# A fused attention block on one core: TensorE's stages in another order, products with v in pairs, and q and k rotated before they are divided by their roots

## The chip, the core and the metric

The kernel runs on one core of one Trainium2 chip. Its engines work side by side, each through its own queue in order, and wait for one another by semaphores: TensorE (PE, with its weight loads as PEld), VectorE (DVE), ScalarE (ACT), GpSimd (POOL) and SyncE (SP), which issues DMAs. The metric is the device time in microseconds (us); lower is better.

## The reference

For 16 sequences of 512 rows with 512 channels, `x` gets an attention branch added. EPS is 1e-6 and there are 16 heads of e = 32 channels.

```python
h = _layernorm(x)
mod = jax.nn.silu(time) @ mod_w + mod_b
shift, scale, gate = jnp.split(mod, 3, axis=-1)
h = h * (scale + 1.0) + shift
qkv = (h @ w_qkv).reshape(B, T, 3, H, e).transpose(2, 0, 3, 1, 4)
q, k, v = (qkv[0], qkv[1], qkv[2])
q = _apply_rope(_layernorm(q, q_norm_w), position)
k = _apply_rope(_layernorm(k, k_norm_w), position)
scores = jnp.einsum('bhqe,bhke->bhqk', q, k) / jnp.sqrt(jnp.asarray(e, q.dtype))
attn = jax.nn.softmax(scores, axis=-1)
o = jnp.einsum('bhqk,bhke->bhqe', attn, v)
o = o.transpose(0, 2, 1, 3).reshape(B, T, D)
return x + o @ w_out * gate
```

Only the first half of each head's channels is rotated by `_apply_rope`.

## The kernel before

The work is cut in two ways. A tile `n` (0 to 63) is 128 rows of one sequence; a group `g` (0 to 63) is 4 heads of one sequence, so a sequence has 4 tiles and 4 groups. There is no scheduler: each engine's program is a loop over stages `s` = 0 to 63, written out by hand, and semaphore counts tie the engines together. Stage `s` works on group `s` by key, on group `s + 1` by query, on tiles ahead and on a tile behind:

- `transpose_c`, `transpose_qk`: the maxima of group `s`, and q and k of group `s + 1`, turned on PE.
- `scores_by_key(s, t)`, t = 0 to 3 (here key(t)): 16 matmuls on row quarters of the array (32 rows each, four at a time) into the banks SA and SM. ACT takes the exponentials from SM first and then from SA (`key_exponentials`, two halves).
- `scores_by_query(s + 1, t)` (here query(t)): 4 such matmuls into SM and MB; DVE takes the maxima of SM, then of MB (`maxima`). SM is shared by query(t) and key(t), so query(t) waits for the first half of the exponentials of key(t), and key(t + 1) waits for the first maximum of query(t).
- `weigh_values(s, t)` (here value(t)): v times the exponentials, on column quarters of the array (128 rows by 32 columns, four at a time) into O. `add_over_keys(s - 1)` (here sums) has the same form, with ones for v, into Y. Each is four matmuls that the trace shows as eight records.
- `project`: q and k of tile `s + 6`, v of tile `s + 4`, 12 matmuls each with the full array, into the one bank Y; `project_out(s - 5)`: the output product, 12 full matmuls, also into Y. `transpose_x(s + 6)` turns the next input tile into SA; ACT and DVE split it in a high and a low part (`x_high`, `x_low`), and key(2), which writes SA next, waits for them.
- For q and k, ACT copies the projection (`move_qk`) and squares it (`square`); DVE sums the squares (`square_sums`), finds the inverse roots and multiplies (`normalize_qk`); then POOL rotates the result (`rotate`, three operations for q and three for k).
- The exponentials are summed over key tiles by two accumulating DMAs, issued by POOL (`add_keys(s, 1)`, `add_keys(s, 3)`), and one POOL addition (`sum_keys(s - 1)`), which the sums on PE then use.

In PE's stage a product with v stands behind each `scores_by_key`, and projections are cut so that a few of their matmuls stand ahead of each `scores_by_query`. In the last stages (`late(s + 1)`, which holds for s from 58 to 62) nothing is left to project for q and k, and the scores by query are made in halves that use MB alone:

```python
if late(s + 1):
    scores_by_query_half(s + 1, 3, 0)
weigh_values(s, 2)
```

There the sums take two parts of the exponentials on PE, and POOL has no `sum_keys`; from group 60 on a spare buffer for them is used (`homes`).

## Time and profile before

| | us |
|---|---|
| median of 3 runs | 1730.7 |
| lowest and highest run | 1730.56, 1736.18 |
| the profiled execution | 1735.34 |
| its span, first to last instruction | 1733.5 |
| PE busy in it | 1660.1 (96%) |
| DVE busy | 1178.0 (68%) |
| ACT busy | 996.9 (58%) |
| POOL busy | 949.5 (55%) |

Busy time of PE is the union of its matmuls' records. A wait between two of them, or a gap that nothing explains, doesn't always show as idle time, since a record's end reaches over the next one's start; so the argument below goes by the distance from one start to the next.

### The profile page before, as it was taken

The page shows a single profiled execution, that of the slowest core. Times are in us where ns is not written, and L with a number is a line of the kernel's source. Part 1 is how long each engine was busy: PE and PEld are TensorE (multiplying, and loading weights), DVE is VectorE, ACT ScalarE, POOL GpSimd, SP SyncE. Part 2 cuts the span into 40 slices and gives each one's busy share as a digit, 9 for nine tenths or more (in the row PEclk, how much of TensorE's full clock was granted, in tenths as well). Part 3 has the DMA queues.
Part 4 walks back from the last instruction along what each step waited for, and adds up shares of the span by engine and source line. Part 5 has one row for each costly group of instructions (what it writes and reads, how often), then busy time and mean ns, then how long its engine had stood idle before and what let it go on. Part 6 is the DMA issues. An engine that isn't in the chain of part 4 may idle for free.

```text
span 1733.5 us, 31073 instructions
## 1 busy us (share of the span) xinstructions
PE 1660.1 (96%) x11870; PEld 955.4 (55%) x11870; DVE 1178.0 (68%) x1541; ACT 996.9 (58%) x1484; POOL 949.5 (55%) x766
## 2 busy tenths in 40 slices
PE   5979999999999999999999999999999999999887
PEld 2745555555555555555555555555555555554434
DVE  8767766676776677666677667667666767765552
ACT  3446666556656655656655665565665566565542
POOL 0535656656565665665665656566566565655322
PEclk9989999999999999999999999999999999999999
DMA  6035454555555555555555454554645546454543
GB/s 214 26 68 110 112 117 107 129 122 122 122 116 125 119 123 124 114 122 128 123 116 135 105 133 116 119 132 106 146 108 116 134 104 140 110 113 107 116 104 110
DMA packets 55417, 204.26 MB, mean 118 GB/s; under 512 B 6872, under 2 KB 6872, under 8 KB 39144
## 3 DMA queue, kind: packets, MB, share of 16 engines
q0 software_dynamic: 18144, 132.13, 38.5%
q1 hardware_dynamic: 37128, 70.14, 12.2%
q8 instruction: 98, 1.61, 0.4%
q14 instruction: 47, 0.39, 0.1%
HBM read 53.25 MB, written 16.88 MB: 40 GB/s over the span
## 4 chain that ended last, share of the span: by engine, by line
PE 82%; DVE 12%; issue 3%; DMA 1%; ACT 1%; POOL 1%; SPq 0%; DVEq 0%; POOLq 0%; ACTq 0%
PE O L481 13%; PE SA L462 12%; PE Y L374 9%; PE Y L370 9%; PE Y L367 9%; DVE cst L1088 6%; PE SM L419 6%; PE Y L496 4%; PE Y L358 4%; PE MB L402 3%; PE Y L380 3%; PE SA L466 2%; DVE hT_lo L1071 2%; PE SM L462 1%; PE SA L440 1%
## 5 line engine op out<-in xcount | busy, mean ns | idle before, releaser
L1088 DVE TENSOR_REDUCE cst<-SM 128x2 fp32r<-128x1024 f32 x236 | 289.4, 1226 | 321.9 <-PE MB L419 321.9
L1334 POOL TENSOR_TENSOR probs<-probs 128x2048 f32<-128x2048 f32 x59 | 271.3, 4599 | 253.4 <-DMA probs<-probs 253.4
L844 ACT ACTIVATE probs<-SM 128x1024 f32<-128x1024 f32 x253 | 259.3, 1025 | 243.6 <-PE SM L466 236.8
L1307 POOL TENSOR_TENSOR pair_part<-rows,rope_pair 128x256 f32<-128x256 f32 x128 | 120.0, 938 | 318.4 <-DVE rows L1065 317.5
L1088 DVE TENSOR_REDUCE cst<-MB 128x2 fp32r<-128x1024 f32 x236 | 287.1, 1216 | 0.0
L481 PE MATMUL O<-probs,vals 128*32 128x512 f32 x2024 | 271.5, 608 | 0.0
L846 ACT ACTIVATE probs<-SA 128x1024 f32<-128x1024 f32 x253 | 257.9, 1019 | 0.0
L741 ACT ACTIVATE rows<-Y 128x512 f32<-128x512 f32 x121 | 72.5, 599 | 232.9 <-PE Y L374 232.9
L370 PE MATMUL Y<-wqkv_hi,hT_lo 128*128 128x512 f32 x716 | 194.3, 393 | 0.4 <-DVE hT_lo L1071 0.4
L374 PE MATMUL Y<-wqkv_lo,hT_hi 128*128 128x512 f32 x716 | 193.2, 391 | 0.0
L1077 DVE SCALAR_TENSOR_TENSOR qk_lo<-MB,pass_w,qk_hi 128x512 fp32r<-128x512 f32 x128 | 90.5, 747 | 131.2 <-ACT qk_hi L777 131.1
L367 PE MATMUL Y<-wqkv_hi,hT_hi 128*128 128x512 f32 x540 | 174.2, 431 | 0.0
L1326 POOL DMA_DIRECT2D probs<-probs x123 | 107.5, 874 | 116.6 <-ACT probs L846 100.1
L370 PEld LDWEIGHTS Y<-wqkv_hi,hT_lo 128*128 128x128 f32 x716 | 134.2, 188 | 32.7 <-DVE hT_lo L1071 0.8
L374 PEld LDWEIGHTS Y<-wqkv_lo,hT_hi 128*128 128x128 f32 x716 | 134.4, 188 | 30.2
L462 PE MATMUL SA<-qk_hi 32*128 32x512 f32 x512 | 128.7, 495 | 20.1 <-DVE hT_lo L1071 11.2
L462 PE MATMUL SM<-qk_hi 32*128 32x512 f32 x512 | 128.3, 497 | 0.0
L419 PE MATMUL SM<-qk_hi 32*128 32x512 f32 x472 | 119.1, 499 | 7.1 <-DVE cst L1088 4.8
L1312 POOL TENSOR_TENSOR rows<-rows,rope_same 128x256 f32<-128x256 f32 x128 | 114.2, 892 | 10.0
L419 PE MATMUL MB<-qk_hi 32*128 32x512 f32 x472 | 118.8, 500 | 0.0
L367 PEld LDWEIGHTS Y<-wqkv_hi,hT_hi 128*128 128x128 f32 x540 | 87.5, 188 | 53.3 <-issue 43.9
L419 PEld LDWEIGHTS SM<-qk_hi 32*128 32x128 f32 x472 | 44.0, 182 | 117.4 <-issue 111.9
(236 smaller groups left out, 3573.2 us busy)
## 6 DMA issues: line engine op xcount, KB each, us to landing
probs<-probs POOLq DMA_DIRECT2D x123, 1024.0 KB, 7.7
xin<-in_x_dram SPq DMA_DIRECT2D x62, 256.0 KB, 7.5
xres<-in_x_dram SPq DMA_DIRECT2D x60, 256.0 KB, 2.6
out_dram<-xres SPq DMA_DIRECT2D x60, 256.0 KB, 5.4
shift_scale<-mod_rows SPq DMA_DIRECT2D x15, 512.0 KB, 3.8
gate<-mod_rows SPq DMA_DIRECT2D x16, 256.0 KB, 5.9
rows<-in_L_cond_mod_w_dram SPq DMA_DIRECT2D x2, 1024.0 KB, 8.9
probs<-in_L_cond_w_qkv_dram SPq DMA_DIRECT2D x2, 1024.0 KB, 13.2
```

The lines of the kernel that those rows point to most:

```text
L367: pe.matmul(bank, x_hi[:, k, :], wqkv_hi[:, k, cols], start=(k == 0), stop=False)
L370: pe.matmul(bank, x_lo[:, k, :], wqkv_hi[:, k, cols], start=False, stop=False)
L374: mm = pe.matmul(bank, x_hi[:, k, :], wqkv_lo[:, k, cols], start=False, stop=(k == DT - 1))
L419: mm = pe.matmul(qm_bank(i), qk_hi[r, g % 2, 0, cols], qk_hi[r, g % 2, 1, :], start=True, stop=True)
L462: pe.matmul(s_bank(i), a[r, ring, 1, cols], c[r, ring, 0, :], start=(a is qk_hi and c is qk_hi), stop=False)
L481: mm = pe.matmul(O[head_rows(i), :], vals[:, b % 2, t, E * h:E * (h + 1)], key_probs(g, t)[:, i, :], start=(t == 0), stop=(t == TT - 1), s ...
L844: act.activation(a[:, 2:4, :], SM[:], ACT.Exp).then_inc(s_exp, 1)
L846: act.activation(a[:, 0:2, :], SA[:], ACT.Exp).then_inc(s_exp, 1)
L1088: dve.tensor_reduce(heads[:, 2 * half:2 * half + 2, 0], bank[:], AX.X, ALU.max, negate=True).then_inc(max_out, 1)
L1307: pool.tensor_tensor(pair_part[:].rearrange("p h (i two) -> p h i two", two=2), swapped, rope_pair[:, t, j, :].rearrange("p (i two) -> p i ...
L1312: pool.tensor_tensor(r[:, :, 0:R], r[:, :, 0:R], rope_same[:, t, j, :].unsqueeze(1) .to_broadcast([P, H, R]), ALU.mult).then_inc(rope_step, 1)
L1334: pool.tensor_tensor(total, total, part, ALU.add).then_inc(keys_summed, 1)
```

## The change

On PE, for stages up to 57, value(0) and value(1) now stand one behind the other with the sums right behind them, and value(2) and value(3) stand together near the end of the stage; value(3) no longer waits for the next stage. The output product is no longer cut: its 12 matmuls and then `transpose_x` follow key(1), ahead of query(1). The v and q projections are cut after 5 of 12 matmuls, the k projection after 8. Stages from 58 on make the scores by query in one piece into SM and MB, as all other stages do; the halves, the spare buffer and the Y bank for `transpose_x` are gone, and only groups 62 and 63 have their sums in more than one part.

POOL rotates q as soon as its squares are taken (`squared`), and DVE's `normalize_qk` waits for the rotation, where POOL had waited for `normalize_qk`. `transpose_qk` waits for `qk_norm`. On POOL, `rotate(s + 5, 0)` stands ahead of `sum_keys(s - 1)`, `rotate(s + 5, 1)` behind it, and then `add_keys(s, 1)`. On DVE the gate's product stands ahead of the maxima of query(1), and `x_low` between these. On ACT `log_sums` stands ahead of the exponentials of key(2).

```diff
+    def late(s):
+        return s > NT - 7
...
+            def project_part(n, j, bank, first, last):
                 x_hi, x_lo = x_buffers(n)
                 cols = slice(j * D, (j + 1) * D)
+                for m in range(first, last):
+                    k, (x, w) = m % DT, ((x_hi, wqkv_hi), (x_lo, wqkv_hi), (x_hi, wqkv_lo))[m // DT]
+                    mm = pe.matmul(bank, x[:, k, :], w[:, k, cols], start=(m == 0), stop=(m == 3 * DT - 1))
+                if last == 3 * DT:
+                    mm.then_inc((q_done, k_done, v_done)[j], 1)
...
             def transpose_qk(g, j):
                 b, i = g // NG, g % NG
                 if i == 0:
-                    pe.wait_ge(rope_step, 6 * (TT * b + 3) + 3 * (j + 1))
+                    pe.wait_ge(qk_norm, TT * b + TT)
...
+                begun = 5 if s > 0 and not late(s - 1) else 0
+                if begun:
+                    project_part(s + 4, 2, Y[:], 0, begun)
+                if group(s + 1):
                     scores_by_query(s + 1, 0)
...
+                        pe.wait_ge(o_low, n + 1)
                         pe.wait_ge(v_out, s + 5)
+                        project_out(n, Y[:], 0, 12)
+                        transpose_x(s + 6)
+                        scores_by_query(s + 1, 1)
...
+                    weigh_values(s, 0)
+                    weigh_values(s, 1)
+                    if s > 0:
...
+                        add_over_keys(s - 1)
...
+                    pe.wait_ge(h_hi, s + 7)
+                    pe.wait_ge(h_lo, s + 7)
+                    project_part(s + 6, 0, Y[:], 0, 5)
+                    scores_by_query(s + 1, 2)
+                    project_part(s + 6, 0, Y[:], 5, 12)
...
                     pe.wait_ge(raw_out, raw_count(s + 6, 0))
+                    project_part(s + 6, 1, Y[:], 0, 8)
                     scores_by_query(s + 1, 3)
+                    weigh_values(s, 2)
+                    weigh_values(s, 3)
+                    project_part(s + 6, 1, Y[:], 8, 12)
...
             def normalize_qk(n):
                 dve.wait_ge(newton_step, NEWTON * (n + 1))
-                dve.wait_ge(squared, 2 * n + 2)
+                dve.wait_ge(rope_step, 6 * (n + 1))
...
             def rotate(n, j):
-                pool.wait_ge(qk_norm, n + 1)
+
+                pool.wait_ge(squared, 2 * n + j + 1)
...
-                if s > 0 and not late(s - 1):
-                    sum_keys(s - 1)
-                add_keys(s, 1)
                 if tile(s + 5):
                     rotate(s + 5, 0)
                 if s > 0:
-                    scale_o(s - 1)
+                    sum_keys(s - 1)
                 if tile(s + 5):
                     rotate(s + 5, 1)
+                add_keys(s, 1)
+                if s - 5 >= 0 and not late(s):
+                    add_residual(s - 5)
+                if s > 0:
+                    scale_o(s - 1)
```

The lists below give the order in which an engine's instructions are queued (line, operation, output and inputs, number of instructions). First PE in a steady stage, from the end of key(3) (L466) to the next stage's transposes (L440, after the change L406). Before, L481 is a product with v, L358, L367, L370 and L374 are the k projection, L419 is query(3):

```order
L466 MATMUL SM<-cT,ones_r 128x512 x2
L481 MATMUL O<-probs,vals 32x512 x4
L358 MATMUL Y<-wqkv_hi,hT_hi 128x512
L419 MATMUL SM<-qk_hi 128x512 x2
L419 MATMUL MB<-qk_hi 128x512 x2
L367 MATMUL Y<-wqkv_hi,hT_hi 128x512 x3
L370 MATMUL Y<-wqkv_hi,hT_lo 128x512 x4
L374 MATMUL Y<-wqkv_lo,hT_hi 128x512 x4
L440 MATMUL SA<-ident_r,cst 128x128 x4
```

The same place after the change, where L432 is the end of key(3), L339 any projection, L396 a query and L447 a product with v:

```order
L432 MATMUL SM<-cT,ones_r 128x512 x2
L339 MATMUL Y<-wqkv_hi,hT_hi 128x512 x4
L339 MATMUL Y<-wqkv_hi,hT_lo 128x512 x4
L396 MATMUL SM<-qk_hi 128x512 x2
L396 MATMUL MB<-qk_hi 128x512 x2
L447 MATMUL O<-probs,vals 32x512 x8
L339 MATMUL Y<-wqkv_lo,hT_hi 128x512 x4
L406 MATMUL SA<-ident_r,cst 128x128 x4
```

One block of eight products with v stands behind query(3), and four matmuls of the k projection behind that, where eleven had been. The second place is PE in the same stage from the output product to key(2), after the change (L357 output product, L331 `transpose_x`, L462 sums, L428 key(2)):

```order
L357 MATMUL Y<-wout_hi,o_lo 128x512
L331 MATMUL SA<-ident,xin 128x128 x4
L396 MATMUL SM<-qk_hi 128x512 x2
L396 MATMUL MB<-qk_hi 128x512 x2
L447 MATMUL O<-probs,vals 32x512 x8
L462 MATMUL Y<-probs,ones_r 32x512 x4
L428 MATMUL SA<-qk_hi 128x512 x2
```

Before, the input's transposes stood inside the output product with eight of its matmuls behind them, then came key(2), and the sums and value(1) behind it. The third place is POOL's queue in one steady stage. Before (L1334 `sum_keys`, L1326 an accumulating DMA, L1307, L1312 and L1315 a rotation, L1340 `scale_o`, L1320 the residual, L1345 `output_low`):

```order
L1334 TENSOR_TENSOR probs<-probs 128x2048
L1326 DMA probs<-probs 128x2048
L1307 TENSOR_TENSOR pair_part<-rows,rope_pair 128x256
L1312 TENSOR_TENSOR rows<-rows,rope_same 128x16x16
L1315 TENSOR_TENSOR rows<-rows,pair_part 128x16x16
L1340 TENSOR_TENSOR oT<-oT,sum_inv 128x4x128
L1307 TENSOR_TENSOR pair_part<-rows,rope_pair 128x256
L1312 TENSOR_TENSOR rows<-rows,rope_same 128x16x16
L1315 TENSOR_TENSOR rows<-rows,pair_part 128x16x16
L1326 DMA probs<-probs 128x2048
L1320 TENSOR_TENSOR xres<-xres,gated 128x512
L1345 TENSOR_TENSOR o_lo<-oT,o_hi 128x512
```

And after the change (rotation L1261, L1266, L1269; `sum_keys` L1288; DMA L1280; residual L1274; `scale_o` L1294; `output_low` L1299):

```order
L1261 TENSOR_TENSOR pair_part<-rows,rope_pair 128x256
L1266 TENSOR_TENSOR rows<-rows,rope_same 128x16x16
L1269 TENSOR_TENSOR rows<-rows,pair_part 128x16x16
L1288 TENSOR_TENSOR probs<-probs 128x2048
L1261 TENSOR_TENSOR pair_part<-rows,rope_pair 128x256
L1266 TENSOR_TENSOR rows<-rows,rope_same 128x16x16
L1269 TENSOR_TENSOR rows<-rows,pair_part 128x16x16
L1280 DMA probs<-probs 128x2048
L1274 TENSOR_TENSOR xres<-xres,gated 128x512
L1294 TENSOR_TENSOR oT<-oT,sum_inv 128x4x128
L1280 DMA probs<-probs 128x2048
L1299 TENSOR_TENSOR o_lo<-oT,o_hi 128x512
```

A rotation now stands on either side of `sum_keys`, and the first DMA issue behind both rotations.

## Rows read from the trace of the kernel before

**Rows 1.** Windows: length, busy of PE, PEld, DVE, ACT, POOL; PE clock; DMA share; GB/s

```profile
217.30:1571.90 1354.60, 1343.44 (x9754) 778.12 (x9753) 938.94 (x1215) 816.05 (x1219) 808.75 (x637) 1.00 0.53 120
1642.91:1669.06 26.15, 22.43 (x153) 10.27 (x153) 11.91 (x11) 11.69 (x15) 5.59 (x6) 0.80 0.46 102
1692.20:1733.50 41.30, 31.68 (x217) 17.48 (x215) 12.46 (x17) 11.71 (x15) 7.57 (x6) 0.91 0.37 109
```

**Rows 2.** Timeline of PE, stage 31: start us, length, what, idle before

```profile
907.40 0.46 PE L440 MATMUL SA<-ident_r,cst 128*128 128x128 f32 x4
...
908.74 0.50 PE L462 MATMUL SA<-qk_hi 32*128 32x512 f32 x2
...
909.88 1.06 PE L481 MATMUL O<-probs,vals 128*32 128x512 f32 x8
910.88 0.73 PE L358 MATMUL Y<-wqkv_hi,hT_hi 128*128 128x512 f32 x2
911.54 0.50 PE L419 MATMUL SM<-qk_hi 32*128 32x512 f32 x2
...
911.98 0.74 PE L367 MATMUL Y<-wqkv_hi,hT_hi 128*128 128x512 f32 x2
...
917.25 0.50 PE L419 MATMUL SM<-qk_hi 32*128 32x512 f32 x2
...
918.26 0.60 PE L350 MATMUL SA<-ident,xin 128*128 128x128 f32 x4
918.61 0.48 PE L380 MATMUL Y<-wout_lo,o_hi 128*128 128x512 f32 x1
918.93 0.40 PE L380 MATMUL Y<-wout_hi,o_lo 128*128 128x512 f32 x1
...
920.32 0.39 PE L380 MATMUL Y<-wout_hi,o_lo 128*128 128x512 f32 x1
920.91 0.50 PE L462 MATMUL SA<-qk_hi 32*128 32x512 f32 x2 [0.20 <-DVE hT_lo L1071]
...
922.04 1.07 PE L496 MATMUL Y<-probs,ones_r 128*32 128x512 f32 x8
922.92 1.04 PE L481 MATMUL O<-probs,vals 128*32 128x512 f32 x8
923.89 0.50 PE L419 MATMUL SM<-qk_hi 32*128 32x512 f32 x2
...
932.92 0.29 PE L440 MATMUL SA<-ident_r,cst 128*128 128x128 f32 x2
```

**Rows 3.** Waits of PE from 217 to 1571 us: us in total, times, longest

```profile
PE SA L462 <- DVE hT_lo L1071: 11.2, 53, 0.2
```

**Rows 4.** Timeline of ACT and DVE, stage 31; line L1065's durations (ns min/median/max)

```profile
909.99 1.02 ACT L844 ACTIVATE probs<-SM 128x1024 f32<-128x1024 f32 x1
910.91 1.02 ACT L846 ACTIVATE probs<-SA 128x1024 f32<-128x1024 f32 x1
...
912.10 1.23 DVE L1088 TENSOR_REDUCE cst<-SM 128x2 fp32r<-128x1024 f32 x1 [0.81 <-PE MB L419]
913.24 1.22 DVE L1088 TENSOR_REDUCE cst<-MB 128x2 fp32r<-128x1024 f32 x1
...
L1065 DVE TENSOR_TENSOR rows<-rows,rstd x64: 1224/1224/1227, 48.0 to 1589.1; 128x1024 f32<-128x1024 f32 x64
```

**Rows 5.** Timeline of POOL in stage 31, and line L1307's durations (ns min/median/max)

```profile
905.25 0.87 POOL L1326 DMA_DIRECT2D probs<-probs  x1 [0.67 <-ACT probs L846]
...
912.45 4.60 POOL L1334 TENSOR_TENSOR probs<-probs 128x2048 f32<-128x2048 f32 x1 [3.77 <-DMA probs<-probs]
...
L1307 POOL TENSOR_TENSOR pair_part<-rows,rope_pair x128: 725/740/1194, 49.4 to 1594.0; 128x256 f32<-128x256 f32 x128
```

**Rows 6.** Timeline of PE in the last stages

```profile
1642.91 0.46 PE L440 MATMUL SA<-ident_r,cst 128*128 128x128 f32 x3 [1.33 <-DVE cst L1096]
...
1702.45 0.70 PE L380 MATMUL Y<-wout_hi,o_lo 128*128 128x512 f32 x1 [2.12 <-POOL o_lo L1345]
```

More of the change, by code:

```diff
@@ L48, in group, with probs_buffer @@
         return 0 <= g < NS
-    def late(g):
-        return group(g) and g > NT - 6
-    homes, spare = [(0, 1, 2, 3)], TT
-    for g in range(1, NS):
-        b = homes[-1]
-        if g < NS - NG:
-            homes.append((b[1], b[3], b[0], b[2]))
-        else:
-            homes.append((spare, b[1], b[3], b[0]))
-            spare = b[2]
+    def late(s):
+        return s > NT - 7
+    PROBS_RING = (0, 1, 3, 2)
+    def probs_buffer(g, t):
+        return PROBS_RING[(PROBS_RING.index(t) + g) % TT]
     def raw_count(n, j):
@@ L420, in scores_by_query @@
                 mm.then_inc(qm_done, 1)
-            def scores_by_query_half(g, t, half):
-                n = TT * g + t
-                if t == 0 and half == 0:
-                    pe.wait_ge(qk_low, 2 * g + 2)
-                pe.wait_ge(max_out, 2 * n + half)
-                cols = slice(t * P, (t + 1) * P)
-                for i in range(2):
-                    r = head_rows(2 * half + i)
-                    mm = pe.matmul(MB[:, i, :], qk_hi[r, g % 2, 0, cols], qk_hi[r, g % 2, 1, :], start=True, stop=True)
-                mm.then_inc(qm_half, 1)
             def transpose_c(g):
@@ L451, in scores_by_key @@
                     pe.wait_ge(s_exp, 2 * n)
-                if t == 0 or (group(g + 1) and not late(g + 1)):
+                if t == 0 or group(g + 1):
                     pe.wait_ge(max_out, 2 * (n + TT - 1) + 1)
-                if t == 2 and g >= 5 and tile(g + 6):
+                if t == 2 and tile(g + 6):
                     pe.wait_ge(h_hi, g + 7)
@@ L586, in _ @@
                 scores_by_key(s, 0)
-                if s > 0:
+                if late(s - 1):
                     weigh_values(s - 1, 3)
@@ L932, in _ @@
                     guess_roots(s + 7)
+                if s > 0 and (s == LAST or not late(s)):
+                    log_sums(s - 1, Y[:])
                 key_exponentials(s, 2, 0)
-                if s > 0:
+                key_exponentials(s, 2, 1)
+                if late(s) and s < LAST:
                     log_sums(s - 1, Y[:])
-                key_exponentials(s, 2, 1)
                 if s > 0:
@@ L1079, in low_qk, with maximum @@
                                          ).then_inc(qk_low, 1)
-            def maxima(g, t):
+            def maximum(g, t, half):
                 dve.wait_ge(qm_done, TT * g + t + 1)
@@ L1086, in maxima @@
                 heads = cst[:, t, :].rearrange("p (h e) -> p h e", e=E)
[L1087 to L1096 removed]
+                dve.tensor_reduce(heads[:, 2 * half:2 * half + 2, 0], (SM, MB)[half][:], AX.X, ALU.max, negate=True
                                   ).then_inc(max_out, 1)
+            def maxima(g, t):
+                maximum(g, t, 0)
+                maximum(g, t, 1)
             def apply_gate(n, bank, to):
@@ L1367, in _ @@
                 if s > 0:
-                    scale_o(s - 1)
+                    sum_keys(s - 1)
                 if tile(s + 5):
                     rotate(s + 5, 1)
+                add_keys(s, 1)
+                if s - 5 >= 0 and not late(s):
+                    add_residual(s - 5)
+                if s > 0:
+                    scale_o(s - 1)
+                if late(s):
+                    add_residual(s - 5)
                 if s == LAST - 1:
```

244 lines of the change are left out of this document (91 added, 153 removed).

## The prediction

> **What bounds the kernel now.** I read the windows by stage first. From 217.3 to 1571.9 us run stages 5 to 57, 53 stages with all parts: 1354.6 / 53 = 25.56 us each, PE busy 1343.4 of 1354.6 us, its granted clock 1.00, DVE at 69%, ACT and POOL at 60% [rows 1]. PE sets the pace, and a stage is worth what its matmuls take plus what lies between them. So I read PE's timeline by distances between starts [rows 2]. Twelve transposes take 1.34 us (907.40 to 908.74), a scores-by-key block 1.14 (to 909.88), one product with v that stands alone 1.00 (to 910.88), two full matmuls between two blocks of other shape 0.66 (to 911.54), a scores-by-query block 0.44 (to 911.98). Seven output matmuls in a row begin from 918.93 to 920.32, 0.23 each. So two full ones cost 2 x 0.23 + 0.20: a run of full matmuls pays 0.20 for its two edges, of which the first interval shows 0.09 (918.61 to 918.93). The sums followed by value(1) show that a column block costs 0.88 when another follows (922.04 to 922.92), not 1.00; with a query behind it, 0.97. The list of waits says that in these 53 stages PE waits for one thing only: key(2) for `x_low`, 11.2 us in 53 times [rows 3]. Around it, 920.32 to 920.91 is 0.59; less 0.23 and a closing edge of 0.09 leaves 0.27 for that wait [rows 2].
>
> The last stages are different. Stages 58 to 62 take 120.3 us (1571.9 to 1692.2), stage 63 with the close 41.3 [rows 1]. PE idles there: 1.33 us before a stage's transposes for the maxima of a half query, 2.12 us in stage 63 for POOL's `output_low` [rows 6]. In stage 61, behind such idle time, the granted clock averages 0.80, so 40% of the stage is at 1.2 instead of 2.4 GHz, and the stage takes 26.15 us where stage 62 takes 23.1 with one output product more [rows 1].
>
> **The change, steady stages.** The number of matmuls stays. What changes are the edges and one wait.
>
> - Column blocks: five pieces (four products and the sums) stand in four groups now, in two after. Two more pieces cost 0.88 instead of 1.00: 0.23 gained. That a piece in a pair costs 0.88 is read from sums then value; value then value writes the same bank O and isn't in the rows: bounds 0 and 0.24.
> - Runs of full matmuls: seven before, seven after (v 5 and 7, output 12 with the turned input, q 5 and 7, k 8, k 4 with the transposes). No gain.
> - The turned input: it stands inside the output product before, 918.26 to 918.93 for four transposes and a matmul, so 0.44. At the end of the run it costs four times 0.11 (1.34 / 12) and perhaps a second edge: I take 0.05 lost, bounds 0 and 0.10.
> - The wait for `x_low`: the turned input now has query(1), both values and the sums behind it before key(2), 3.1 us. ACT's and DVE's halves of it took until 0.2 past the need with eight output matmuls (2.3 us) as cover, and half a query's maxima stand ahead of it instead of a whole query's. 0.27 gained, bounds 0.20 and 0.28.
>
> Sum: 0.23 - 0.05 + 0.27 = 0.45 a stage, 25.1 us, times 53 = 24 us. With the bounds it is 5 to 29.
>
> **What hides the rest.** A stage after, from its transposes: key(0) 1.3, query(0) 3.8, key(1) 6.1, output 7.2, turned input 10.1, query(1) 10.7, value(0) 11.1, sums 12.9, key(2) 13.8, query(2) 16.3, key(3) 18.6, query(3) 21.7, value(2) 22.2, rest of k 24.1, end 25.1. The waits that could take hold:
>
> - query(0) and query(2) need SM's exponentials, 2.27 us after the key's start (908.74 to 909.99 + 1.02) [rows 2, 4]. The key and five matmuls take 1.14 + 5 x 0.23 + 0.20 = 2.49: 0.2 to spare, less than now, where the product with v stands there.
> - The next transposes need both maxima of query(3), 2.92 us after its start (911.54 to 913.24 + 1.22) [rows 2, 4]; it has 0.44 + 0.88 + 1.00 + 1.02 = 3.3. Key(3) needs the first maximum of query(2), 1.8 after 16.3, so 18.1 against 18.6. If these covers were 0.5 us shorter each, each would cost the difference.
> - POOL. The second DMA is issued when value(2) is done, at 23.2, and lands 7.2 us on (905.25 to 912.45) [rows 5], at 5.4 of the next stage; `sum_keys` 4.6 us ends at 10.0; the k rotation, three operations of about 0.8, at 12.5. The sums on PE want it at 12.9 from `sum_keys` alone, 2.9 to spare. DVE wants the rotation for `normalize_qk`: now 4.9 us after query(1) (917.25 to 922.12, where its 1.22 us start); after, at about 15.0. So 2.5 to spare. It then ends at 16.2, ahead of query(2)'s maxima at 16.9. The q rotation lies at the stage's start, before the DMA lands. The first DMA is issued at about 12.5 and is needed by the next stage's exponentials at 27.7; the residual, `scale_o` and the second issue follow with room. SP's stores hang on the residual, which comes earlier than now.
>
> Stages 0 to 4 lack the output product, so query(1) waits for exponentials in the new order too; the idle time moves and I count 0 to 1 us gained. At the start the rotations run ahead of the roots instead of behind them, with transposes waiting for the later of the two: 0.
>
> **The change, last stages.** Query pieces whole. From a key's start the query comes at 2.3 (exponentials), and the next key at the earliest 1.84 behind the query (SM's first maximum) [rows 4]. In stages 60 and 61 the output product comes in halves of 6 x 0.23 + 0.20 = 1.58, which cover that for t = 0 and 1: 1.34 + 2 x (2.3 + 0.44 + 1.58) + (2.3 + 1.84) + (2.3 + 2.97) = 19.4. Stages 58 and 59 have a v projection and a whole output product: 21.2 and 22.2. Stage 62 adds an output product that waits for POOL, whose `output_low` is queued behind `scale_o` and the residual: 22. Together 104 instead of 120.3. But each of these stages ends in 2.5 us without a matmul (2.97 less 0.44), longer than today's gap. In today's stage 61 the half clock cost some 3 us for 10 us at 1.2 GHz; I put 8 us on five stages. Stage 63: the output product of tile 59 now stands ahead of key(1) and waits there for the same POOL chain, but the sums are out of the close; 1 to 2 us gained. Sum 120.3 + 41.3 - 104 - 8 - 40 = 10 us gained, bounds 2 (clock down most of the time, stage 63 worse) and 18 (no clock loss).
>
> **Total.** 24 + 10 + 0.5 = 34.5 off the profiled execution's 1735.3 gives 1701. That execution lies 4.6 above the median of the runs, 1730.7; taken off the median, 1696.
>
> **The rivals.**
>
> - *The edges only move.* A product in a pair pays its edge all the same, or the 0.2 us covers fail and give the 0.45 back. Then only the last stages gain: 1720. For it: 0.2 us is thin. Against: 0.88 is measured. Chance 0.10.
> - *The last stages gain nothing*, since PE idles longer and is at 1.2 GHz for most of them: 1730.7 - 24 = 1706. For it: 0.80 in stage 61. Chance 0.10.
> - *Slower: the rotation behind `sum_keys` comes late.* POOL waits for the DMA, then adds, then rotates k, and DVE, in order, holds `normalize_qk` and query(2)'s maxima behind it; key(3) on PE waits. It costs from 3.6 us of delay on (2.5 of POOL, 0.6 on DVE, 0.5 before key(3)), and outweighs the gain 0.65 us later still (0.45 a stage, and 10 / 53 for the tail). With the DMA landing 5 us later than its 7.2, a stage would lose 1.4 - 0.45: 50 - 10 = 40 us, 1771. Against: POOL waits 3.77 us for this DMA today, and nothing on PE shows it. Chance 0.06.
> - *DVE is held up by POOL.* L1307 takes 0.74 us, but up to 1.19 beside some DVE work [rows 5], so the two do touch. In the new order `normalize_qk` at 15.0 meets the residual's addition on POOL. It has 0.6 + 0.5 us to spare; held 1.5 us by it, each stage gives 0.4 back: 1730.7 - 10 - 3 = 1718. Against: L1065 never took over 1.227 us in 64 times [rows 4], though it met few POOL operations. Chance 0.06.
>
> By the Trainium skill, "SBUF — State Buffer", section "Who interferes with whom", a DVE instruction with two SBUF inputs and a GpSimd instruction that reads SBUF exclude each other for the whole of whichever came first; by it this last rival would be the rule, wherever the two meet, and the rotations would get shorter beside maxima, which read PSUM. The trace agrees in that L1307's time varies.
>
> **How the numbers follow.** The forecast has 0.68. The range is 1685 to 1712: it takes in the tail's bounds, a steady gain from 0.25 to 0.55 a stage, and the second rival; the first, third and fourth lie outside. A difference under 0.5% (9 us) can't be told from none by these runs. Faster by more: forecast, second rival, most of the first and fourth, 0.90. Slower: 0.05. Between: 0.05.
>
> **What would show it.** A steady stage of 25.1 us; value(0) to value(1) 0.88; no wait of key(2) for `x_low`; POOL's k rotation ending near 12.5; stages 60 and 61 near 20, with the clock under 1.00. I'd be wrong if query(0) or query(2) waited for ACT in each stage, if DVE waited for `rope_step`, or if the last stages ran at 1.2 GHz throughout.

## The result and the profile after

The changed kernel takes 1721.36 us (median of 5 runs, 1719.39 to 1723.68) against 1732.28 for the kernel before (5 runs): ratio 0.9937, 95% interval 0.9921 to 0.9954. It is faster by 0.6%, where 2% was forecast, and 1721 lies above the range's end of 1712. The profiled execution spans 1719.1 us against 1733.5.

The same stretches as in [rows 1], from the windows of the changed kernel. The first window runs over stages 5 to 57, the next over stage 61, then stage 62, then stage 63 with the close, the last over stages 58 to 63 together. Columns: length, busy of PE, PEld, DVE, ACT, POOL, PE clock, DMA share, GB/s.

```profile
227.25:1561.39 1334.14, 1327.30 (x9753) 788.32 (x9752) 969.92 (x1215) 815.52 (x1219) 773.93 (x637) 1.00 0.54 123
1624.45:1645.69 21.24, 17.68 (x144) 8.56 (x144) 11.53 (x12) 11.85 (x15) 10.07 (x6) 0.92 0.67 143
1651.43:1676.66 25.23, 22.07 (x156) 12.48 (x157) 11.53 (x11) 11.86 (x15) 10.26 (x7) 0.86 0.60 126
1676.66:1719.10 42.44, 32.33 (x217) 18.07 (x215) 12.45 (x17) 11.70 (x15) 7.56 (x6) 0.89 0.29 90
...
1561.39:1719.10 157.71, 129.54 (x965) 68.48 (x963) 74.00 (x79) 73.59 (x96) 63.22 (x43) 0.90 0.49 112
```

Stages 5 to 57 begin at 227.25 instead of 217.30 [rows 1]. So three parts make up the difference: everything ahead of stage 5 became 10.0 us longer, the 53 steady stages 20.5 shorter (1354.60 to 1334.14), the last stages with the close 3.9 shorter (120.3 + 41.3 to 157.7). That is -14.4. Nearly 1 us of this only changed place: value(3) now stands in its own stage, so stage 0 holds eight records of products with v more (32 for 24) and stage 58 eight fewer.

**The steady stages.** Most of them do what was forecast. This is PE's timeline of stage 22 (start us, length, what), the counterpart of [rows 2].

```profile
652.66 0.46 PE L406 MATMUL SA<-ident_r,cst 128*128 128x128 f32 x4
...
662.52 0.40 PE L357 MATMUL Y<-wout_hi,o_lo 128*128 128x512 f32 x1
662.75 0.60 PE L331 MATMUL SA<-ident,xin 128*128 128x128 f32 x4
663.29 0.49 PE L396 MATMUL SM<-qk_hi 32*128 32x512 f32 x2
...
663.72 1.92 PE L447 MATMUL O<-probs,vals 128*32 128x512 f32 x16
665.46 1.04 PE L462 MATMUL Y<-probs,ones_r 128*32 128x512 f32 x8
666.43 0.50 PE L428 MATMUL SA<-qk_hi 32*128 32x512 f32 x2
...
677.68 0.46 PE L406 MATMUL SA<-ident_r,cst 128*128 128x128 f32 x4
```

The stage is 25.02 long. Two products with v take 1.74 (663.72 to 665.46), 0.87 each, and key(2) at 666.43 carries no idle time. But 11 of the 53 stages are longer than 25.2, up to 26.24; their excess over 25.02 is 7.6 us, and 8.1 over all 53. The waits of PE in these stages name what comes late: the maxima, ahead of a key block, 11 times.

```profile
PE SA L428 <- DVE cst L1053: 6.8, 11, 1.1
```

What holds the maxima is seen on DVE and POOL. The timeline of stage 22 first (25.02), then of stage 23 (25.77):

```profile
665.99 1.58 POOL L1274 TENSOR_TENSOR xres<-xres,gated 128x512 f32<-128x512 f32 x1
666.71 0.91 DVE L1000 TENSOR_SCALAR half_var<-stats 128x33 f32<-128x33 f32 x1
...
668.21 1.22 DVE L1031 TENSOR_TENSOR rows<-rows,rstd 128x1024 f32<-128x1024 f32 x1
...
685.01 4.62 POOL L1288 TENSOR_TENSOR probs<-probs 128x2048 f32<-128x2048 f32 x1 [4.05 <-DMA probs<-probs]
...
692.12 2.02 DVE L1004 TENSOR_TENSOR newton<-newton,half_var 128x33 f32<-128x33 f32 x1
692.51 1.58 POOL L1274 TENSOR_TENSOR xres<-xres,gated 128x512 f32<-128x512 f32 x1
...
694.41 1.23 DVE L1031 TENSOR_TENSOR rows<-rows,rstd 128x1024 f32<-128x1024 f32 x1
...
696.92 0.49 PE L428 MATMUL SA<-qk_hi 32*128 32x512 f32 x2 [0.67 <-DVE cst L1053]
```

The root steps work on 128 x 33 numbers and take 0.17 to 0.20 us. L1000 takes 0.91 here, and ends at 667.62 with POOL's residual addition (667.57). In stage 23 the second accumulating DMA lands late, `sum_keys` begins at 7.3 into the stage instead of 5.8, POOL's chain shifts by 1.5, and a later root step, L1004, ends with the residual (694.14 and 694.09) after 2.02. Then `normalize_qk` (L1031) starts at 16.7 into the stage instead of 15.6, query(2)'s maxima are late and key(3) waits 0.67. In ten of the 11 long stages `sum_keys` begins 6.6 to 7.8 into the stage; in stage 30 it is on time (5.8), and the residual is 0.8 late because POOL's first DMA issue waits for value(1).

**The start.** DVE and POOL in the timeline at the preparation of the fourth tile (tile 3), where PE then idles:

```profile
68.52 4.54 POOL L1305 TENSOR_TENSOR wout_lo<-probs,wout_hi 128x2048 fp32r<-128x2048 f32 x1
68.65 4.46 DVE L1006 SCALAR_TENSOR_TENSOR rstd<-newton,rstd 128x33 f32<-128x33 f32 x1
...
75.03 1.22 PE L339 MATMUL Y<-wqkv_hi,hT_lo 128*128 128x512 f32 x2 [4.64 <-DVE hT_lo L1037]
```

The subtraction for `wout_lo` used to begin at 75.24, behind a rotation that waited for this very division. Now nothing holds it back, it begins 0.13 us ahead of the last root step, and the root step ends with it, after 4.46 us. Stage 0's first transposes follow at 102.08 instead of 95.84. Stages 0 and 1 then take 27.64 and 25.59 instead of 25.46 and 24.0. In stage 1 the granted clock is 0.93 where it was 1.00. In stage 0 it is no lower than before (0.76 and 0.75), though it is at half in places (the window below); there value(3) accounts for nearly 1 us, and the rest of the 2.2 isn't taken apart.

```profile
98.50:105.30 6.80, 4.02 (x24) 3.12 (x28) 3.34 (x5) 1.97 (x3) 0.00 (x0) 0.50 0.00 0
```

### The profile page after: what moved, and what is told of

Read it like the earlier page. It is cut to its first block, busy times and chain, and to the rows that moved or that the text cites. A ratio compares the mean times of both kernels' runs of the same rounds, so it can differ in the third digit from the quotient of the medians.

```text
span 1719.1 us, 31069 instructions
## 1 busy us (share of the span) xinstructions
PE 1641.9 (96%) x11846; PEld 967.8 (56%) x11846; DVE 1210.6 (70%) x1541; ACT 997.1 (58%) x1484; POOL 926.3 (54%) x769
## 4 chain that ended last, share of the span: by engine, by line
PE 83%; DVE 8%; issue 4%; DMA 3%; POOL 1%; ACT 1%; SPq 0%; POOLq 0%; ACTq 0%; DVEq 0%
PE Y L339 31%; PE O L447 12%; PE SA L428 12%; PE Y L357 10%; PE SM L396 6%; PE MB L379 3%; PE SA L432 3%; PE Y L462 2%; DVE cst L1053 2%; PE SA L331 2%; DMA probs<-probs 1%; DVE newton L1004 1%; PE SA L406 1%; DVE rows L1031 1%; DMA probs<-in_L_cond_w_qkv_dram 1%
## 5 line engine op out<-in xcount | busy, mean ns | idle before, releaser
L1053 DVE TENSOR_REDUCE cst<-SM 128x2 fp32r<-128x1024 f32 x256 | 313.7, 1225 | 183.5 <-PE MB L396 183.0
L1288 POOL TENSOR_TENSOR probs<-probs 128x2048 f32<-128x2048 f32 x62 | 285.4, 4604 | 200.1 <-DMA probs<-probs 200.1
L1053 DVE TENSOR_REDUCE cst<-MB 128x2 fp32r<-128x1024 f32 x256 | 311.3, 1216 | 0.0
L1280 POOL DMA_DIRECT2D probs<-probs x126 | 110.1, 873 | 308.9 <-PE O L447 298.5
L447 PE MATMUL O<-probs,vals 128*32 128x512 f32 x2048 | 253.9, 610 | 0.0
L339 PE MATMUL Y<-wqkv_hi,hT_lo 128*128 128x512 f32 x716 | 226.8, 412 | 4.6 <-DVE hT_lo L1037 4.6
L339 PE MATMUL Y<-wqkv_hi,hT_hi 128*128 128x512 f32 x716 | 213.5, 420 | 0.0
L339 PE MATMUL Y<-wqkv_lo,hT_hi 128*128 128x512 f32 x716 | 202.0, 404 | 0.0
L1294 POOL TENSOR_TENSOR oT<-oT,sum_inv 128x512 f32<-128x512 f32 x63 | 83.5, 1326 | 169.5 <-ACT sum_inv L781 169.5
L339 PEld LDWEIGHTS Y<-wqkv_lo,hT_hi 128*128 128x128 f32 x716 | 130.4, 188 | 75.7 <-issue 48.6
L339 PEld LDWEIGHTS Y<-wqkv_hi,hT_hi 128*128 128x128 f32 x716 | 120.5, 188 | 81.4 <-issue 28.7
L339 PEld LDWEIGHTS Y<-wqkv_hi,hT_lo 128*128 128x128 f32 x716 | 126.0, 189 | 55.4 <-issue 28.5
L1261 POOL TENSOR_TENSOR pair_part<-rows,rope_pair 128x256 f32<-128x256 f32 x128 | 113.5, 886 | 69.0 <-ACT squares L723 68.6
L396 PE MATMUL SM<-qk_hi 32*128 32x512 f32 x512 | 128.6, 497 | 15.9 <-ACT probs L808 11.0
L428 PE MATMUL SA<-qk_hi 32*128 32x512 f32 x512 | 129.1, 500 | 11.7 <-DVE cst L1053 11.0
L1066 DVE TENSOR_TENSOR gated<-Y,gate 128x512 f32<-128x512 f32 x60 | 41.5, 691 | 128.8 <-PE Y L357 128.8
L428 PE MATMUL SM<-qk_hi 32*128 32x512 f32 x512 | 129.1, 501 | 0.0
L396 PE MATMUL MB<-qk_hi 32*128 32x512 f32 x512 | 128.8, 498 | 0.0
```

Of the source, the lines that this page charges most:

```text
L339: mm = pe.matmul(bank, x[:, k, :], w[:, k, cols], start=(m == 0), stop=(m == 3 * DT - 1))
L396: mm = pe.matmul(qm_bank(i), qk_hi[r, g % 2, 0, cols], qk_hi[r, g % 2, 1, :], start=True, stop=True)
L428: pe.matmul(s_bank(i), a[r, ring, 1, cols], c[r, ring, 0, :], start=(a is qk_hi and c is qk_hi), stop=False)
L447: mm = pe.matmul(O[head_rows(i), :], vals[:, b % 2, t, E * h:E * (h + 1)], probs[:, probs_buffer(g, t), i, :], start=(t == 0), stop=(t == ...
L1053: dve.tensor_reduce(heads[:, 2 * half:2 * half + 2, 0], (SM, MB)[half][:], AX.X, ALU.max, negate=True).then_inc(max_out, 1)
L1261: pool.tensor_tensor(pair_part[:].rearrange("p h (i two) -> p h i two", two=2), swapped, rope_pair[:, t, j, :].rearrange("p (i two) -> p i ...
```

## The experiments

The theory: the order on PE is right; what took back the gain is the other half of the change, the rotation ahead of the division, which puts POOL operations with two SBUF inputs beside DVE's root steps. The main rival: the rotation ahead of the division makes the roots late by itself, or the late DMA does. The table splits each profiled execution at stage 0's first transpose and at the starts of stages 5 and 58 (us; "longer than 25.2" counts steady stages, "rest" is stages 58 to 63 with the close). Each row is one execution: where the code is the same, the parts still differ by up to 1.4 us in the first five stages and 3.5 in the last ones.

| | stage 0 at | stage 5 at | stages 5-57 | longer than 25.2 | rest | span |
|---|---|---|---|---|---|---|
| before | 95.8 | 217.3 | 1354.6 | all | 161.6 | 1733.5 |
| after | 102.1 | 227.3 | 1334.1 | 11 | 157.7 | 1719.1 |
| e1_wout | 98.8 | 222.5 | 1335.4 | 13 | 154.2 | 1712.1 |
| e2_residual | 103.2 | 226.2 | 1328.2 | 2 | 157.8 | 1712.2 |
| e3_both | 97.9 | 220.5 | 1328.3 | 3 | 156.3 | 1705.1 |
| e4_order | 96.2 | 220.3 | 1325.1 | 0 | 157.5 | 1702.9 |
| e5_rotation | 103.4 | 224.1 | 1354.1 | all | 158.4 | 1736.6 |
| e6_unpair | 95.7 | 223.1 | 1347.9 | all | 158.1 | 1729.1 |
| e7_tail | 95.7 | 221.0 | 1326.5 | 0 | 150.2 | 1697.8 |
| e8_pieces | 100.5 | 223.4 | 1336.9 | 13 | 156.0 | 1716.3 |

### e1_wout: the subtraction for wout_lo one rotation later

```diff
             for n in range(5):
+                rotate(n, 0)
                 if n == 4:
                     pool.wait_ge(wout_high, 1)
                     pool.tensor_tensor(wout_lo[:], ...).then_inc(wout_low, 1)
-                rotate(n, 0)
                 rotate(n, 1)
```

> The changed kernel with one operation moved: the subtraction that makes the low part of the output weights (wout_lo, 4.5 us on POOL) stands between the two rotations of stage 4's tile and not ahead of both. Theory (the start is late because this subtraction now runs beside VectorE's root step of tile 3 and holds it for 4.46 us): the root step is back near 0.2 us, the first keys' transpose starts near 96 instead of 102.1, TensorE keeps its clock there, and the span is 6 to 10 us below the changed kernel's 1719.1, thus 1709 to 1713. Rival (the start is late because the rotation ahead of the division puts the roots later, whatever stands beside them): the first transpose stays near 102 and the span stays at 1718 to 1720. Steady stages as in the changed kernel by both.

Measured 1715.21 us, ratio 0.9897 (0.9877 to 0.9916), span 7.0 below the changed kernel's, as the theory had it; the rival, by which the first transpose stays near 102, falls. The root step L1006 of tile 3 is back at 0.20 us, and L1006 never takes more than 0.783. Stage 0 begins at 98.75, 3.3 earlier, though not at 96: rotations still stand beside root steps. For tile 4:

```profile
85.39 0.76 DVE L1004 TENSOR_TENSOR newton<-newton,half_var 128x33 f32<-128x33 f32 x1
86.19 0.78 DVE L1006 SCALAR_TENSOR_TENSOR rstd<-newton,rstd 128x33 f32<-128x33 f32 x1
87.01 1.81 DVE L1031 TENSOR_TENSOR rows<-rows,rstd 128x1024 f32<-128x1024 f32 x1
```

The kernel before has 0.20, 0.20 and 1.22 there. Of the 7.0 us, 4.7 lie ahead of stage 5 and 3.5 in the last stages, less 1.2 in the steady ones. The 3.5 was not foreseen, and the code of these stages is the same: stage 59 takes 22.75 at a granted clock of 0.99 (25.29 at 0.87 in the changed kernel) and stage 61 takes 20.0 at 0.98 (21.2 at 0.92). Why one execution keeps its clock there and another doesn't is open.

### e2_residual: the residual addition behind the scaling

```diff
-                if s - 5 >= 0 and not late(s):
-                    add_residual(s - 5)
                 if s > 0:
                     scale_o(s - 1)
-                if late(s):
+                if s - 5 >= 0:
                     add_residual(s - 5)
```

> The changed kernel with the residual addition of every stage behind the scaling of the outputs on POOL, not ahead of it. Theory (the residual addition, which reads two tiles from SBUF for 1.6 us, runs beside VectorE's small steps of the roots; each then lasts about as long as it does, and where the sum over the keys is late, this holds normalize_qk until 16.7 us into the stage, so that the stage is 0.4 to 1.2 us too long): the first root step is back at 0.17 us, normalize_qk starts near 14.9 into the stage, all steady stages are 25.02, and the 53 of them take 8 us less, 1326 instead of 1334; span near 1711. Rival (the late landing of the second keys' transfer alone delays the chain, through sum_keys and the second rotation): stages of 25.8 remain in the same number, and the 53 stages stay within 2 us of 1334. A second one: VectorE is then late with something else that the scaling of the outputs or the addition runs beside, and the stages are longer than 25.02 throughout. The start stays late by both (first keys' transpose at 102).

Measured 1714.43 us, ratio 0.9889 (0.9862 to 0.9916). The steady stages take 1328.2, 5.9 less (8 were expected). The list of L1000's durations (ns, min/median/max) in the changed kernel, then here:

```profile
L1000 DVE TENSOR_SCALAR half_var<-stats x64: 172/916/1842, 45.9 to 1574.0; 128x33 f32<-128x33 f32 x64
```

```profile
L1000 DVE TENSOR_SCALAR half_var<-stats x64: 172/174/544, 45.9 to 1567.1; 128x33 f32<-128x33 f32 x64
```

The DMA lands late in ten stages here that are 25.02 long all the same (`sum_keys` begins 7.1 to 7.5 us into the stage): in stage 23, for one, it begins at 7.5, and `normalize_qk` at 15.1. All 11 long stages of the changed kernel are 25.02 now. So landing that late does no harm without the residual, which decides against the rival there. Two other stages are long, 37 (26.17) and 41 (25.95), where `sum_keys` begins at 9.1 and 8.9, but the delay doesn't come by way of the rotation. The timeline of stage 37, which begins at 1026.85:

```profile
1035.93 1.03 ACT L808 ACTIVATE probs<-SM 128x1024 f32<-128x1024 f32 x1 [2.29 <-DMA probs<-probs]
1035.96 4.57 POOL L1288 TENSOR_TENSOR probs<-probs 128x2048 f32<-128x2048 f32 x1 [5.86 <-DMA probs<-probs]
...
1038.01 0.63 PE L331 MATMUL SA<-ident,xin 128*128 128x128 f32 x4 [0.92 <-ACT probs L810]
```

The exponentials of key(1) wait for the same DMA as `sum_keys`, and `transpose_x`, which overwrites SA once they have read it, waits on PE. It starts 11.16 into the stage instead of 10.09, so nearly all of the stage's 1.15 us is lost ahead of query(1), before `normalize_qk` comes (16.3, late with the rest). A DMA that lands about 3 us late costs the stage even so, by way of ACT.

### e3_both: both moves

> Both moves at once: the low part of the output weights between the two rotations of stage 4, and the residual addition behind the scaling of the outputs. Theory (both faults are the same kind of meeting of POOL and VectorE, at different places, so they add): span 14 to 18 us below the changed kernel's 1719.1, thus 1701 to 1705, 0.984 of the kernel before. Rival (either is not the cause): the gains of the two single runs, added, whatever they are; if each is 0, 1719.

Measured 1708.39 us, ratio 0.9859 (0.9839 to 0.9880), span 14.0 below the changed kernel's: the two single spans gained 7.0 and 6.9. The span is at the upper end of what was expected; the median lies 3 us above it. Three stages are long, and PE waits in them as in stage 37 of e2.

### e4_order: the order on PE alone, the rotation behind the division

```diff
 # POOL, rotate
-                pool.wait_ge(squared, 2 * n + j + 1)
+                pool.wait_ge(qk_norm, n + 1)
 # DVE, normalize_qk
-                dve.wait_ge(rope_step, 6 * (n + 1))
+                dve.wait_ge(squared, 2 * n + 2)
 # POOL, stage s
-                if tile(s + 5):
-                    rotate(s + 5, 0)
                 if s > 0:
                     sum_keys(s - 1)
-                if tile(s + 5):
-                    rotate(s + 5, 1)
                 add_keys(s, 1)
-                if s - 5 >= 0 and not late(s):
-                    add_residual(s - 5)
+                if tile(s + 5):
+                    rotate(s + 5, 0)
                 if s > 0:
                     scale_o(s - 1)
...
```

The transposes of q and k wait for the rotation again, and the second rotation and the residual stand where the kernel before has them.

> The changed kernel with the order on TensorE (products with v in pairs) kept, and the rotation put back behind the division by the roots, with POOL's order of before. This parts the change into its halves. Theory (the pairs bring the shorter stage; the rotation ahead only cost: the late start, and the long stages): the start is as before (first keys' transpose near 96), and the steady stages are 25.0 to 25.1 throughout, so that the span is near 1702 to 1706. Rival (the pairs bring only the column block, 0.23 a stage, and the rotation ahead is what takes away the wait for the maxima or for the keys, 0.27 a stage): steady stages near 25.3, span about 1716 to 1720.

Measured 1704.79 us, ratio 0.9839 (0.9816 to 0.9862), where both halves together have 0.9937. All 53 stages are 25.0, though the DMA lands late in seven of them (`sum_keys` at 7.3 to 7.7), and the windows show PE busy for the whole of them:

```profile
220.30:1545.38 1325.08, 1325.08 (x9754) 787.23 (x9752) 958.82 (x1215) 816.45 (x1219) 809.38 (x636) 1.00 0.54 123
```

PE's order alone gives 29.5 us in the steady stages. Ahead of stage 5 it costs 3.0, not by its start (96.2) but in stage 0, 27.88 instead of 25.46: nearly 1 us is value(3), the granted clock of the stage is 0.70 (0.75 before), and query(1) waits 1.2 us for exponentials, which no output product covers there. How the rest divides isn't measured.

### e5_rotation: the rotation ahead, in the kernel before

The same edit the other way round, on the kernel before; PE's order stays.

> The kernel before with the other half of the change alone: q and k are rotated ahead of the division by the roots, POOL's rotations move accordingly, and TensorE's order is that of before. Theory (the rotation ahead only costs): the start is late by 6 to 10 us because VectorE's root step stands beside the subtraction for wout_lo, the steady stages stay at 25.56, and the time is 1737 to 1742, ratio 1.003 to 1.006. Rival (the rotation ahead brings something in the steady stages that only the pairs' order hides): steady stages below 25.4, time below 1731. A third way, by which the addition of the residual was only harmful because of its new place ahead of the scaling: steady stages without any long one.

Measured 1737.67 us, ratio 1.0038 (1.0023 to 1.0054). Stage 0 begins at 103.4, the longest root step (here L1040) is 4.456 us, the steady stages are unchanged (1354.1), and nothing is gained by the rotation ahead. The residual keeps its old place, and no stage is long though the DMA lands late in some of them. So this half costs some 7 us alone (6.8 ahead of stage 5, 7.9 by the medians); beside PE's new order, with the residual moved ahead, it costs 16 (spans 1719.1 and 1702.9). The last stages take 158.4 here and 161.6 in the kernel before, whose code is the same from stage 59 on. The difference is stage 61: 21.7 at a granted clock of 1.00, where the kernel before's profiled execution had 26.1 at 0.80 [rows 1].

### e6_unpair: value(1) out of its pair, on e4_order

```diff
                     weigh_values(s, 0)
-                    weigh_values(s, 1)
                     ...
                 else:
+                    weigh_values(s, 1)
                     if s > 0:
                         pe.wait_ge(sum_ln, s)
```

> The changed TensorE order with the rotation behind the division (the variant that is the fastest so far, steady stages 25.00), in which value(1) is taken out of its pair and stands alone behind key(2). Three groups of products with v instead of two. Theory (each group's edge costs 0.12 us): steady stages 25.12 to 25.2, the 53 of them 6 to 8 us longer than the 1325.1 of that variant, and value(1) alone takes 0.99 and the rest of its old group 1.85. Rival (the pair saves nothing, since the two write the same bank; what shortened the stage is the covered wait for x_low): 25.00 as before, 0 us. A second rival: query(2) gets more cover and key(2) less, so that the wait for x_low comes back and the stage grows by 0.3 or more.

Measured 1730.86 us, ratio 0.9993 (0.9983 to 1.0004): all of the gain is gone with one move. A steady stage is 25.42. PE's timeline of stage 22 and its waits:

```profile
666.12 1.06 PE L447 MATMUL O<-probs,vals 128*32 128x512 f32 x8
667.00 1.04 PE L462 MATMUL Y<-probs,ones_r 128*32 128x512 f32 x8
668.21 0.49 PE L428 MATMUL SA<-qk_hi 32*128 32x512 f32 x2 [0.17 <-DVE hT_lo L1037]
```

```profile
PE SA L428 <- DVE hT_lo L1037: 7.5, 46, 0.2
```

Here 667.00 to 668.21 is 1.21, where the pair's order has 0.97 between the same two: 0.24 of wait. Of the other 0.18, value(1) alone, which takes 0.99 instead of 0.87, makes the edge's 0.12. So the theory's edge and the second rival's wait are both there, and the theory's 25.12 to 25.2 was too low for want of the wait. Of the 26.2 us between the spans, the 53 stages account for 22.8 and what lies ahead of them for 2.8. The rival that a pair saves nothing falls.

### e7_tail: e4_order with two moves in the last stage

```diff
 # POOL, last stage
-                    add_residual(NT - TT - 2)
                     output_low(NT - TT - 1)
+                    add_residual(NT - TT - 2)
 # PE, last stage: output product of tile 59
-                    pe.wait_ge(o_low, NT - TT)
-                    pe.wait_ge(y_gated, NT - TT - 1)
-                    project_out(NT - TT - 1, Y[:], 0, 12)
                 scores_by_key(s, 1)
                     ...
                         add_last_sums(0)
+                        pe.wait_ge(o_low, NT - TT)
+                        pe.wait_ge(y_gated, NT - TT - 1)
+                        project_out(NT - TT - 1, Y[:], 0, 12)
```

> The variant with the changed TensorE order and the rotation behind the division, and in the last stage two moves: POOL makes the low part of the output of tile 59 ahead of the addition of the residual of tile 58, which waits 8.25 us for its load, and TensorE takes that output product behind key(1), value(0) and the last sums of t = 0 instead of ahead of key(1). Theory (the output product waits for POOL, which stands at the residual's load; 6.8 us idle, then the clock at 1.2 GHz): the wait of 6.8 us goes, the clock stays higher, and the time is 6 to 9 us below that variant's 1704.8, thus 1696 to 1699. Rival (the load of x for the residual, or VectorE's gated product behind it, is what the end hangs on, so the wait moves to the last products): the gain is under 2 us.

Measured 1699.32 us, ratio 0.9810 (0.9790 to 0.9830), the fastest here, 5.5 below e4_order. The timelines of both, e4_order first: POOL stands at the residual's load, PE behind it, and the product then runs at half clock (0.43 between starts instead of 0.23).

```profile
1665.05 1.26 POOL L1274 TENSOR_TENSOR xres<-xres,gated 128x512 f32<-128x512 f32 x1 [8.25 <-DMA xres<-in_x_dram]
1666.26 1.26 POOL L1299 TENSOR_TENSOR o_lo<-oT,o_hi 128x512 fp32r<-128x512 f32 x1
...
1667.58 0.79 PE L357 MATMUL Y<-wout_hi,o_hi 128*128 128x512 f32 x1 [6.77 <-POOL o_lo L1299]
1668.17 0.63 PE L357 MATMUL Y<-wout_lo,o_hi 128*128 128x512 f32 x1
1668.60 0.63 PE L357 MATMUL Y<-wout_hi,o_lo 128*128 128x512 f32 x1
```

```profile
1663.88 0.50 PE L428 MATMUL SA<-qk_hi 32*128 32x512 f32 x2 [1.05 <-ACT probs L811]
...
1666.87 0.50 PE L357 MATMUL Y<-wout_hi,o_hi 128*128 128x512 f32 x1
1667.20 0.40 PE L357 MATMUL Y<-wout_lo,o_hi 128*128 128x512 f32 x1
1667.44 0.39 PE L357 MATMUL Y<-wout_hi,o_lo 128*128 128x512 f32 x1
```

The last part falls from 157.5 to 150.2; the rival, under 2 us, falls. The start and the steady stages are 2.2 us longer than e4_order's, which this edit doesn't touch; that is the difference between two executions of the same code, and hence 5.5 and not 7.

### e8_pieces: the same POOL work, in pieces

```diff
-                    pool.tensor_tensor(wout_lo[:], wout_raw, wout_hi[:].bitcast(F32), ALU.subtract
-                                       ).then_inc(wout_low, 1)
+                    for i in range(DT):
+                        piece = pool.tensor_tensor(wout_lo[:, i], wout_raw[:, i], wout_hi[:, i].bitcast(F32),
+                                                   ALU.subtract)
+                    piece.then_inc(wout_low, 1)
-                pool.tensor_tensor(xres[:], xres[:], gated[:], ALU.add).then_inc(res_added, 1)
+                h = D // 2
+                pool.tensor_tensor(xres[:, 0:h], xres[:, 0:h], gated[:, 0:h], ALU.add)
+                pool.tensor_tensor(xres[:, h:D], xres[:, h:D], gated[:, h:D], ALU.add).then_inc(res_added, 1)
```

> The changed kernel, nothing moved, but POOL does the subtraction for wout_lo in four pieces of a quarter each and the addition of the residual in two halves, at the same places. Theory (POOL's operation with two SBUF inputs shuts out VectorE's for the whole of its own duration, and lets it in at its end): the root step of tile 3, 4.46 us beside the whole subtraction, ends with the piece that it met, so at most 1.3 us, and the root steps in the steady stages fall from 0.92 to under 0.8, the longest from 2.04 to about 1; the first keys' transpose is 2 to 3 us earlier than 102.1, and the long stages get shorter. Rival (the two engines share the reads' bandwidth, so the small step is slow as long as POOL reads at all): the root step still takes about 4.5 us and stage lengths are as in the changed kernel.

Measured 1720.88 us, ratio 0.9937 (0.9913 to 0.9961). The two halves of the expectation fare differently. The timeline at `wout_lo` (four pieces in one row) and of a steady stage:

```profile
69.02 6.39 POOL L1308 TENSOR_TENSOR wout_lo<-probs,wout_hi 128x512 fp32r<-128x512 f32 x4
69.15 1.20 DVE L1006 SCALAR_TENSOR_TENSOR rstd<-newton,rstd 128x33 f32<-128x33 f32 x1
70.38 2.22 DVE L1031 TENSOR_TENSOR rows<-rows,rstd 128x1024 f32<-128x1024 f32 x1
...
662.66 1.03 POOL L1275 TENSOR_TENSOR xres<-xres,gated 128x256 f32<-128x256 f32 x1
663.35 1.03 POOL L1276 TENSOR_TENSOR xres<-xres,gated 128x256 f32<-128x256 f32 x1
663.38 1.04 DVE L1000 TENSOR_SCALAR half_var<-stats 128x33 f32<-128x33 f32 x1
```

At `wout_lo`, the root step is held 1.20 instead of 4.46: DVE gets in near the end of the first piece, so here it was shut out by the instruction and not slowed by POOL's traffic, and stage 0 begins 1.6 earlier. The steady stages got no better (1336.9), against the expectation. L1000 takes 1.05 in the median, not under 0.8, and the longest root step 2.25, not about 1. In the stage above, the step starts 0.03 behind the second half's start and ends with it. Where it starts sooner, it is held through both halves, as in stage 23:

```profile
688.82 2.17 DVE L1004 TENSOR_TENSOR newton<-newton,half_var 128x33 f32<-128x33 f32 x1
689.20 1.03 POOL L1275 TENSOR_TENSOR xres<-xres,gated 128x256 f32<-128x256 f32 x1
689.89 1.03 POOL L1276 TENSOR_TENSOR xres<-xres,gated 128x256 f32<-128x256 f32 x1
```

So it goes with all 31 root steps that start ahead of the second half and meet the addition: none ends between the halves. That DVE is let in at the end of each POOL instruction is shown for `wout_lo` alone; in the steady stages the two halves hold it like one, the rival's stage lengths came true, and why is open.

## Why the prediction was wrong

The direction was right, the size was not: 34.5 us were forecast off the profiled execution, 14.4 came. Of the 20.1 missing, 10.5 are the start, 3.5 the steady stages, 6.1 the last ones. The other 5 us between 1696 and 1721.4 come from the baseline: with two more runs the kernel before's median was 1732.3 instead of 1730.7, and medians moved by 10.9, less than the two profiled executions. The kernel before's profiled execution, 4.6 above the median, spent 3.2 us more in its last stages than e5's, whose code is the same from stage 59 on.

- **The start: the failed step is "At the start the rotations run ahead of the roots instead of behind them, with transposes waiting for the later of the two: 0."** It looked at what waits for the rotations and not at what the rotations used to hold back on POOL. `wout_lo` was queued behind rotations that waited for `normalize_qk`; freed of that wait it meets the root step, and stage 0 begins 6.2 us later. The runs show it from both sides: what lies ahead of stage 5 gets shorter by 4.7 us in e1, 6.7 in e3 and 7.0 in e4, and 6.8 longer when the rotation ahead is put into the kernel before (e5). The "0 to 1 us gained" of stages 0 to 4 failed too: they became 3.7 longer. That isn't the meeting: e4 and e7, without it, are 2.6 and 3.8 longer over them. Nearly 1 us is value(3); the lack of cover and the clock are my reading of the rest.
- **The rival "DVE is held up by POOL" (0.06, 1718) had the mechanism**, but at the wrong place and with the wrong sum; that 1718, or the 1720 of the first rival, lies near 1721 is luck. It had 0.4 given back in each of 53 stages, 21 us, and nothing at the start; the long stages gave back 7.6 in all, and the meeting at the start cost 6.2. I looked for it at `normalize_qk`, which takes 1.22 here too in the median, and took L1065's narrow range as evidence against; that row holds only instructions which met little of POOL. The ones hit are the root steps just ahead of it. In 42 stages this is hidden by the spare time; in ten of the other 11 it adds to a late DMA. e2 shows that with the residual moved away all 11 are back at 25.02. The Trainium skill, "SBUF — State Buffer", section "Who interferes with whom", says that of DVE and GpSimd the first to issue keeps the pair of ports that they share for its whole instruction. The trace agrees with that rule at `wout_lo`: 4.46 us beside one instruction, 1.20 beside the first of four in e8. In e8's steady stages it goes further than the rule: two instructions in a row hold the root step through both, 2.17 us.
- **The rival of a late rotation behind `sum_keys`** was never put to the test: in no run does PE wait by that path alone. Where `sum_keys` was 3.3 and 3.1 us late, in stages 37 and 41 of e2, the stages lost 1.2 and 0.9 by another one, which the prediction left out: the exponentials of key(1) wait for the same DMA.
- **The steady stage** was forecast at 25.1 and is 25.02 (25.00 in e4), 0.54 gained for 0.45. (The bounds of its terms add up to 0.10 to 0.52 a stage, which is 28 us at the top and not 29.) Column blocks give 0.28, not 0.23: before they take 1.00, 1.00, 0.88, 0.97 and 1.00, 4.84 in all by their means; after, 1.74 + 0.97 and 1.85, 4.56. The turned input costs nothing (12 output matmuls, four transposes and their edges take 659.88 to 663.29, 3.41 = 12 x 0.23 + 0.20 + 0.44), where I had put 0.05. The wait for `x_low` went, 0.27. The covers of 0.2 us for the exponentials held. Had all 53 stages been so, the gain would be 28.6; those above 25.02 took 8.1 of it.
- **The last stages: "Sum 120.3 + 41.3 - 104 - 8 - 40 = 10"** came to 3.9. Stages 58 to 62 took 115.3 for 112, and stage 63's 40 was 2.4 short. One step that failed is "Stage 62 adds an output product that waits for POOL ... 22": the stage took 25.2, and PE waits 1.8 us in it and 3.6 in stage 63 for `output_low`. In stage 63 that stands behind a residual addition which waits 8.0 us for its load, and the product behind it then runs at half clock. e7 takes that wait away, 6.8 in e4, and gets 7.3 us. Stage 59 was 3.1 over its 22.2, too; at a clock of 0.99 it takes 22.75 (e1), so 2.5 of that go with the clock, 0.87 here. And the 120.3 was itself high: the stage 61 from which the prediction priced the clock takes 21.7 and not 26.1 in e5. The last stages with the close took 161.6 and 158.4 in the two executions of the old order, and 157.7, 154.2, 157.7 and 156.3 in the four with the changed kernel's; so single executions can't size this part to better than some 3 us, and nearly 1 us of its gain is value(3), which moved ahead.

What stays open: why L1004 in stage 23 is already held from 692.12, 0.39 ahead of the residual's recorded start. It is so in eight of the long stages, each time 0.2 to 0.3 us behind the start of POOL's DMA issue; that issue alone doesn't do it, since in e2 the same step beside it takes 0.20. Open too are what a POOL operation in two halves does to DVE, and when the clock falls in the last stages.

## What to carry to other kernels

When an operation is moved ahead of a wait, list what was queued behind that wait on the same engine: it will now start early, and it is the next suspect. Look for collisions between POOL's long two-input operations and DVE's *short* ones on the critical chain: here a 0.2 us step took 4.5 us, and its maximum in the list of durations shows it at once. Ask of a stage that is priced from one execution whether another execution of the same code has it too. Make and time the two halves of a joint change apart: here one gave 29 us in the steady stages and the other only cost.

## What was not expected of the hardware

- A DVE operation with one SBUF input, the tensor_scalar L1000 on 128 x 33, is held by a POOL operation as well: 916 ns in the median beside the residual addition, 174 when that is moved away (e2).
- POOL's addition in two halves holds a root step through both, up to 2.25 us, in 31 of 31 cases that start ahead of the second half (e8).
- Two products with v in a row into the same bank cost 0.87 us each, no more than a product behind the sums (0.88).
- An unpaired product with v brings back 0.42 us a stage for an edge of 0.12 us, since the time that `x_low` needs was covered by the pair (e6).
